# Layer 1's side work cut into steps of one or two f32 matmuls, beside a fixed 22-step unit of attention

## The chip, the cores and the metric

The kernel runs on one core of one Trainium2 chip. The metric is the device time of one execution in microseconds (us), as a median over runs.

## The reference, cut to what matters

Two layers work on x, 8 batches of 512 rows of 256 numbers. Layer 0 is softmax attention beside a mixture of experts. Layer 1 is two causal attentions with a convolution between them, beside a low-rank feed-forward part. The change is in layer 1's attention:

```python
qkv = x @ Wqkv_w.T + Wqkv_b
q, k, v = (qkv[:, :, 0], qkv[:, :, 1], qkv[:, :, 2])
ctx = _causal_attn(q, k, v)
conv_out = jax.lax.conv_general_dilated(ctx_c, conv_w, window_strides=(1,), padding=[(1, 1)], ...) + conv_b[None, :, None]
q2 = conv_out.transpose(0, 2, 1).reshape(b, s, NUM_HEADS, HEAD_DIM)
ctx2 = _causal_attn(q2, k, v)
out = ctx2.reshape(b, s, d) @ out_w.T + out_b
```

## The kernel before, in words

**Units.** Layer 1 is cut into 32 units, numbered 16 to 47. A unit is one batch, eight of the 16 heads (c = 0 or 1) and one of the two attentions: kind 1 is the first attention, kind 2 the second. The order is two units of kind 1, then two of kind 2, and so on. A unit has two halves (g = 0, 1) of four heads.

**What a unit needs.** Its queries and keys are computed as f32 matmuls (`query_key`, L765; for kind 2 the convolution, L1019, six matmuls of 512 columns) and its values (L773). ScalarE takes the bf16 head of each (`high`, L1607), VectorE the rest (`residue`, L1153), GpSimd splits that once more (L1844, L1846), and SyncE copies the parts by six DMAs into the tall tiles QA and KA (`fan`, L1986). For kind 1 the keys are also stored to DRAM (`ks`), from where kind 2 fans them again.

**The maxima.** The softmax subtracts each row's maximum before its exponentials. So a unit's scores are computed twice: first as packs into the three banks S1 (L804), where VectorE takes the maxima (L1195). The maxima of a half are transposed by TensorE (L811), split into three bf16 rows by VectorE (L1211 to L1219), and SyncE writes the rows into QA by three small DMAs from t_msp. Then the scores are computed again with these rows (L826, and L830 adds the causal mask) into the two banks S2, ScalarE takes the exponentials (L1629), and TensorE multiplies them by the values (`product`, L843) into the bank PV. A half is closed by a copy of PV (L1640), four transposes (L858) and a division (L1245, L1253).

**Stages.** One turn of `pipeline`'s loop, here called a stage, interleaves four lanes on every engine: `expp` of unit i (scores, exponentials, products, closings), `maxp` of unit i + 1 (maxima), `pre1` of unit i + 2 (queries, keys, values, fans), and `fin1` of unit i - 1 (for c = 1 of kind 2: transposes of the context, L724, the output projection, L1045, its addition, L1535, and the store). Every engine walks through the same lanes and emits only its own instructions, in this order; it waits at semaphores. `pre1` comes in every second step, `fin1` in every third. One step of `pre1` holds a whole `query_key`, a whole value projection or a whole convolution. A whole period is four stages, and this text names them by what `pre1` prepares: P and P (units of kind 1), Q (kind 2, c = 0, which has `fin1` beside it) and R (kind 2, c = 1).

**Waits that tie the stages.** TensorE's first pack of a unit waits in `maxp` for both fans of this unit (`d_f`); `pre1` issued them one stage earlier. The first scores of a half wait for the three rows of maxima (`d_mq`). SyncE issues all these DMAs in one order.

## Time and profile before

| | |
|---|---|
| median of 3 runs | 2157.86 us (2154.74 to 2158.21) |
| profiled execution, its own time | 2160.07 us |
| its span | 2158.2 us |
| mean granted TensorE clock | 0.935 |
| TensorE busy, VectorE busy, ScalarE busy | 85%, 58%, 47% of the span |
| layer 1's stages, from the first pack of the first to the end | 1223.5 to 2158.2 us |

The span is the time from the first to the last instruction of one profiled execution. Busy times of TensorE count each matmul to the end of its passage through the array, so that a busy TensorE is not one at its peak.

### The profile page before, as it was taken

What the parts mean: (1) busy time and instruction counts of PE and PEld (TensorE: products, weight loads), DVE (VectorE), ACT (ScalarE), POOL (GpSimd) and SP (SyncE); (2) the same over time, 40 slices, a digit from 0 to 9 for tenths busy, and PEclk for the clock granted to TensorE, in tenths of its full rate; (3) what the DMA queues carried; (4) which work ended last, traced back from release to release, by engine and by line L of the source; (5) the groups of instructions that cost most, each with busy time, mean ns of one, the idle gap of its engine ahead of it and who ended that gap; (6) DMA issues with size and microseconds to landing.
All of it is one profiled execution on the core that took longest, in us unless ns stands there. A gap on an engine that the chain in (4) does not pass through costs nothing.

```text
span 2158.2 us, 31797 instructions
## 1 busy us (share of the span) xinstructions
PE 1836.4 (85%) x10767; PEld 901.2 (42%) x10777; DVE 1255.3 (58%) x3777; ACT 1020.4 (47%) x2048; POOL 363.6 (17%) x555
## 2 busy tenths in 40 slices
PE   3475799999989999995489797998998898889987
PEld 2341344554534454541234343444444444444433
DVE  4554455655555444552554676767676767776663
ACT  0242456555545555564244244544454445445444
POOL 2215221121101111112443101001010100000000
PEclk8557899999999999998599899999999999999999
DMA  7245343434364444423104235555453545554350
GB/s 144 70 141 143 67 80 72 84 72 79 67 171 94 69 62 69 62 33 85 38 22 65 31 53 60 75 70 75 63 74 54 73 67 68 77 68 59 50 60 21
DMA packets 145969, 155.87 MB, mean 72 GB/s; under 512 B 26009, under 2 KB 132785, under 8 KB 145809
## 3 DMA queue, kind: packets, MB, share of 16 engines
q1 hardware_dynamic: 123872, 114.75, 34.0%
q0 software_dynamic: 10048, 14.44, 3.7%
q10 hardware_dynamic: 11888, 24.64, 3.6%
q8 instruction: 88, 1.44, 0.3%
q14 instruction: 73, 0.59, 0.1%
HBM read 55.95 MB, written 33.72 MB: 42 GB/s over the span
## 4 chain that ended last, share of the span: by engine, by line
PE 65%; DVE 15%; ACT 6%; issue 5%; DMA 4%; POOL 4%; SPq 2%; DVEq 0%; ACTq 0%; POOLq 0%
PE p_PV L843 12%; PE p_S L826 9%; PE p_S L804 9%; DVE p_S L1195 6%; PE p_Ma L1019 4%; PE p_Mb L898 4%; PE p_S L921 4%; ACT t_R L1629 3%; PE p_Ma L765 3%; SPq L1986 2%; PE p_Ma L773 2%; PE p_Mb L765 2%; PE p_S L830 2%; POOL idd L1878 1%; PE p_Mb L921 1%
## 5 line engine op out<-in xcount | busy, mean ns | idle before, releaser
L1629 ACT ACTIVATE t_R<-p_S 128x512 f32<-128x512 f32 (+1 forms) x1216 | 670.8, 577 | 503.7 <-PE p_S L830 347.0
L1195 DVE CUSTOM_DVE_ANT_0 p_S<-p_S,t_NM 128x128 f32<-128x128 f32 (+3 forms) x1024 | 472.3, 522 | 90.2 <-PE p_S L804 86.7
L804 PE MATMUL p_S<-t_R 96*128 96x512 bf16 (+3 forms) x1536 | 456.0, 340 | 64.2 <-DVE t_mx L1195 32.2
L1201 DVE TENSOR_REDUCE t_mx<-p_S 128x1 f32<-128x512 f32 x512 | 346.6, 686 | 260.1 <-PE p_S L804 247.0
L826 PE MATMUL p_S<-t_R 99*128 99x512 bf16 (+3 forms) x1536 | 468.4, 332 | 21.9 <-ACT t_R L1629 8.7
L843 PE MATMUL p_PV<-t_R 128*17 128x512 f32 (+3 forms) x3072 | 325.2, 495 | 12.4 <-ACT t_R L1629 10.0
L804 PEld LDWEIGHTS p_S<-t_R 96*128 96x128 bf16 x1536 | 135.8, 99 | 395.2 <-issue 136.5
L826 PEld LDWEIGHTS p_S<-t_R 99*128 99x128 bf16 x1536 | 150.0, 98 | 175.5 <-issue 79.6
L1844 POOL CAST t_spl<-t_rr 128x512 bf16<-128x512 f32 x80 | 49.0, 612 | 969.9 <-DVE t_rr L1153 969.8
L830 PE MATMUL p_S<-t_NM 128*128 128x128 bf16 x1024 | 196.1, 220 | 0.0
L1195 DVE DVE_READ_ACCUMULATOR2_ANT t_mx<- 128x1 f32 x1024 | 145.0, 142 | 0.0
L830 PEld LDWEIGHTS p_S<-t_NM 128*128 128x128 bf16 x1024 | 101.3, 99 | 37.8 <-issue 10.6
L898 PE MATMUL p_Mb<-t_R,t_NM 128*128 x184 | 97.9, 613 | 7.3 <-DMA t_NM<-hTd 3.0
L843 PEld LDWEIGHTS p_PV<-t_R 128*17 128x17 f32 x3072 | 50.9, 95 | 120.7 <-issue 86.1
L921 PE MATMUL p_S<-t_R,t_NM 128*128 x392 | 101.2, 380 | 0.0
L1846 POOL TENSOR_TENSOR t_spl<-t_rr,t_spl 128x512 bf16<-128x512 f32 x80 | 92.5, 1156 | 6.4
L1019 PE MATMUL p_Ma<-t_NM,t_R 128*128 128x512 f32 x192 | 90.4, 622 | 0.0
L921 PEld LDWEIGHTS p_S<-t_R,t_NM 128*128 128x128 f32 x392 | 74.3, 191 | 18.4 <-issue 2.9
L1211 DVE TENSOR_SCALAR t_msp<-p_S 16x128 bf16<-16x128 f32 x96 | 26.7, 278 | 74.6 <-PE p_S L811 71.5
L1902 POOL DMA_DIRECT2D ysd<-t_NM x39 | 34.1, 875 | 210.4 <-ACT t_NM L1688 210.4
L1153 DVE SCALAR_TENSOR_TENSOR t_rr<-p_Ma,t_BQK,t_spl 128x512 f32<-128x512 f32 x32 | 24.0, 751 | 76.2 <-ACT t_spl L1607 76.2
L1716 ACT ACTIVATE t_R<-p_S,t_R 128x512 f32<-128x512 f32 x64 | 43.5, 687 | 50.7 <-PE p_S L967 42.5
(245 smaller groups left out, 2124.1 us busy)
## 6 DMA issues: line engine op xcount, KB each, us to landing
t_R<-t_spl SPq DMA_DIRECT2D x480, 128.0 KB
t_R<-in_w ACTq DMA_DIRECT2D x32, 512.0 KB, 7.6
t_R<-ks SPq DMA_DIRECT2D x96, 128.0 KB
ks<-t_spl SPq DMA_DIRECT2D x16, 384.0 KB, 7.3
hTd<-t_NM SPq DMA_DIRECT2D x39, 128.0 KB
ysd<-t_NM SPq DMA_DIRECT2D x39, 128.0 KB
t_NM<-hTd SPq DMA_DIRECT2D x39, 128.0 KB, 2.3
ysd<-t_NM POOLq DMA_DIRECT2D x39, 128.0 KB, 3.1
```

The source lines that it names most:

```text
L765: t = self.nc.tensor.matmul(M[:, :], m.WQ[:, cc, off:off + 128], xT[:, cc, :], start=(cc == 0), stop=(cc == 1))
L804: t = self.nc.tensor.matmul(bank[:, z, :], qa[0:96, h, qb * 128:(qb + 1) * 128], ka[0:96, h, 0:n], start=True, stop=True)
L826: t = self.nc.tensor.matmul(bank[:, z, :], ka[0:99, h, kb * 128:(kb + 1) * 128], qa[0:99, h, n0:512], start=True, stop=not u.causal)
L830: t = self.nc.tensor.matmul(bank[:, z, 0:128], m.identb, m.maskk, start=False, stop=True)
L843: t = self.nc.tensor.matmul(m.PV[32 * j:32 * j + 17, n0:512], vt[:, kb, 4 * g + j, :], m.P1[kb][j] if u.causal else m.P[p % 2][:, j, :], s ...
L898: z = self.nc.tensor.matmul(m.MB[i][:, :], m.hT[t % 2][:, c, :], m.W1[:, bass.ds(self.regs[t], 1), c, :], start=(c == 0), stop=(c == 1))
L921: x = self.nc.tensor.matmul(M[:, 0:256], m.AT[:, k, :], m.W2[:, bass.ds(self.regs[t], 1), k * 256:k * 256 + 256], start=(k == 0), stop=(p ...
L1019: t = self.nc.tensor.matmul(M[:, :], m.CW[:, i, c * 128:c * 128 + 128], m.cT[:, cc, k:k + 512], start=(i == 0), stop=(i == 5))
L1195: x = nc.vector.tensor_tensor_reduce(out=sc, in0=sc, in1=m.maskq[:, 512 - n:512], scale=1.0, scalar=NEG, op0=ALU.add, op1=ALU.max, accum_o ...
L1201: nc.vector.tensor_reduce(m.mx[:, g, i:i + 1], m.S1[s1_bank(k)][:, :], AX.X, ALU.max).then_inc(s.s1_read, 1)
L1629: nc.scalar.activation(m.P1X[kb][j0 // per] if u.causal else m.P[p % 2][:, j0:j0 + per, :], m.s2_bank(k)[:, 0:per * n].rearrange("p (j n) ...
L1846: g.tensor_tensor(m.spl[:, z, 2, :], m.rr[:, :], m.spl[:, z, 1, :], ALU.subtract).then_inc(s.lo_done, 1)
```

## The change

`pipeline` goes. Now all four lanes take one part in each step, and a stage has 22 steps, one for each exponential: a pack of maxima and a piece of scores in every step. `pre1` starts at its step 3 (first step: 0) for kind 1 and gives one f32 matmul of `query_key` to a step (3, 4 and 6, 7), the value projection's eight small ones two to a step (10 to 13), the convolution's six one to a step (5 to 10 with the transposes ahead of it for c = 0, 3 to 8 for c = 1). `high1`, `rest` and `fan1` follow in the steps behind. The transposition of a half's maxima, its split and its rows (`shift`) come in steps 2 and 3 of the next half, where they stood in step 12 of their own half. The product of a block comes two steps after its last scores (`due`), and a half's closing (`close1`) in steps 2, 4 and 5 of the next half. `fin1` uses one bank for both of its transposes (Mb) and one for both of its projections (Ma). For the first batch of kind 2 and the last, `pre1` starts at step 6 and puts two matmuls of the convolution in a step; the two units that the feed-forward part prepares use the bank S1[2]. No operation is added or taken out.

```diff
-LATE2 = (4, 0, 0, 0, 0, 0, 0, 4)
-LATE = 3
...
+TOPS = {}
+_n = 0
+for _u in UNITS0:
+    for _g in range(2):
+        TOPS[_u.n, _g] = _n + len(packs_of(_u))
+        _n += len(packs_of(_u)) + 1
+for _u in UNITS1:
+    for _g in range(2):
+        _n += len(packs_of(_u))
+        TOPS[_u.n, _g] = _n + 2 * (_u.n - 16) + _g
+
+
+
+def bank_of(u, z):
+
+    return 2 if u.n < 18 else (0, 1, 0)[z]
...
 def layer1(e):
-    pipeline(UNITS1, 0, e.expp, e.maxp, e.pre1, lambda i, lane: [(lane(e.fin1, i - 1), 3)])
+
+    def lane(f, i):
+        return f(UNITS1[i]) if 0 <= i < len(UNITS1) else none()
+    for i in range(len(UNITS1) + 1):
+        interleave([(lane(e.expp, i), 1), (lane(e.maxp, i + 1), 1), (lane(e.pre1, i + 2), 1), (lane(e.fin1, i - 1), 1)])
 
...
-        return steps(s1_uses(u) + 2 * u.causal)
+        return self.maxima(u) if u.causal else self.maxp0(u)
+
+    def maxp0(self, u):
+        return steps(s1_uses(u))
+
+    def maxima(self, u):
+
+        for g in range(2):
+            for qb, js in packs_of(u):
+                self.top(u, g, qb, js)
+                next(self.chain, None)
+                yield
+            self.chain = self.shift(u, g)
+        if u.n == 47:
+            yield from self.chain
+
+    def shift(self, u, g):
+
+        yield
+        yield
+        self.turn_m(u, g)
+        self.split_m(u, g)
+        yield
+        self.rows(u, g)
+        yield
...
-        return steps(3 if u.kind == 1 else 2 if u.c else LATE2[u.b] + 4)
+
+        if u.kind == 1:
+            yield from steps(3)
+            self.part(u, 0, 0)
+            yield
+            self.part(u, 0, 1)
+            yield
+            self.high1(u, 0)
+            yield
+            self.rest(u, 0)
+            self.part(u, 1, 0)
+            yield
+            self.part(u, 1, 1)
+            yield
+            self.fan1(u, 0)
+            self.high1(u, 1)
+            yield
+            self.rest(u, 1)
+            yield
+            for k in range(4):
+                self.part(u, 2, k)
+                if k == 1:
+                    self.fan1(u, 1)
+                yield
+            self.values(u)
+            return
+        soon = u.c or u.b not in (0, NB - 1)
+        yield from steps(3 if u.c else 1 if soon else 6)
+        if u.c == 0:
+            for c in range(2):
+                self.turn_c(u, c)
+                yield
+                self.keep_c(u, c)
+                yield
+        for i in range(6):
+            self.convolve(u, i)
+            if i == 3:
+                self.fan1(u, 1)
+            if soon or i % 2:
+                yield
+        self.high1(u, 0)
+        yield
+        self.rest(u, 0)
+        yield
+        self.fan1(u, 0)
+        yield
...
-        return steps(LATE + 4) if u.kind == 2 and u.c else none()
+
+        if u.kind != 2 or u.c != 1:
+            return
+        yield from steps(6)
+        for c in range(2):
+            self.turn_f(u, c)
+            yield
+            self.keep_f(u, c)
+            yield
+        yield from steps(4)
+        for h in range(2):
+            self.out(u, h)
+            yield
+            self.add_out(u, h)
+            yield
+        self.store(u)
...
+    def exponentials(self, u):
+
+        for g in range(2):
+            for kb in range(4):
+                n0 = 128 * kb
+                per = (1, 1, 2, 4)[kb]
+                for j0 in range(0, 4, per):
+                    self.scores(u, g, kb, j0, per, n0)
+                    self.products()
+                    yield
+                self.due.append([2, u, g, kb])
+        if u.n == 47:
+            for _ in range(8):
+                self.products()
+                yield
+
+    def products(self):
+
+        for d in self.due:
+            d[0] -= 1
+        while self.due and self.due[0][0] == 0:
+            _, u, g, kb = self.due.pop(0)
+            self.product(u, g, kb)
+            if kb == 3:
+                self.closing = self.close1(u, g)
+        next(self.closing, None)
+
+    def close1(self, u, g):
+
+        yield
+        self.copy_o(u, g)
+        yield
+        yield
+        self.turn_o(u, g)
+        yield
+        self.divide(u, g)
+        yield
...
+    def top(self, u, g, qb, js):
+        e, m, s = self.e, self.m, self.s
+        qa, ka = m.QA[u.buf], m.KA[u.buf]
+        e.wait_ge(s.d_f[0][u.buf], 96 * u.fill)
+        e.wait_ge(s.d_f[1][u.buf], 96 * u.fill)
+        n = 128 * (qb + 1)
+        k, self.s1 = self.s1, self.s1 + 1
+        self.s1_free(k)
+        bank = m.S1[s1_bank(k)][:, 0:len(js) * n].rearrange("p (j n) -> p j n", j=len(js))
+        for z, j in enumerate(js):
+            h = 4 * g + j
+            t = self.nc.tensor.matmul(bank[:, z, :], qa[0:96, h, qb * 128:(qb + 1) * 128], ka[0:96, h, 0:n],
+                                      start=True, stop=True)
+        t.then_inc(s.s1_mm, 1)
+
+    def s1_free(self, k):
+
+        e, s = self.e, self.s
+        e.wait_ge(s.s1_read, k - 2 if k >= LAYER1 + 3 else LAYER1)
+        if k == LAYER1 + 1:
+            e.wait_ge(*self.mfree[2])
+        if k == LAYER1 + 2:
+            e.wait_ge(s.qs_done, NB)
+
+    def turn_m(self, u, g):
+        e, m, s = self.e, self.m, self.s
+        k, self.s1 = self.s1, self.s1 + 1
+        if u.causal:
+            self.s1_free(k)
+        e.wait_ge(s.s1_read, TOPS[u.n, g])
+        self.nc.tensor.transpose(m.S1[s1_bank(k)][0:16, 0:128], m.mx[:, g, :], m.ident[:, :]).then_inc(s.s1_mm, 1)
...
+    def part(self, u, z, k):
+        e, m, s, b = self.e, self.m, self.s, u.b
+        xT = m.XT[:, :, 512 * b:512 * b + 512]
+        i = bank_of(u, z)
+        if k == 0:
+            e.wait_ge(s.d_l2, 96)
+            e.wait_ge(s.nT_done, 2 * b + 2)
+            self.mbank(i, *((s.rr_done, QK[u.n, z]) if z < 2 else (s.v_done, VN[1, b, u.c])))
+        M = m.MB[i]
+        if z < 2:
+            off = 256 * z + 128 * u.c
+            t = self.nc.tensor.matmul(M[:, :], m.WQ[:, k, off:off + 128], xT[:, k, :], start=(k == 0), stop=(k == 1))
+            if k == 1:
+                t.then_inc(s.qk_mm, 1)
+        else:
+            off = 512 + 128 * u.c
+            for cc in range(2):
+                t = self.nc.tensor.matmul(
+                    M[:, k * 128:(k + 1) * 128], xT[:, cc, k * 128:(k + 1) * 128], m.WQ[:, cc, off:off + 128],
+                    start=(cc == 0), stop=(cc == 1))
+            if k == 3:
+                t.then_inc(s.v_mm, 1)
...
```

`convolve`, `turn_c`, `keep_c`, `turn_f`, `keep_f`, `out`, `add_out`, `store`, `split_m`, `rows`, `copy_o`, `turn_o`, `divide` hold the instructions of the old `pre1`, `fin1`, `maxp` and `close`.

**TensorE at the start of a stage P.** Before, with the wait for the rows of maxima in the first row (L826 scores, L830 mask, L804 maxima, L765 queries and keys, L843 products):

```order
L826 MATMUL p_S20<-t_R2 128x512 [waits d_mq20]
L830 MATMUL p_S20<-t_NM 128x128
L804 MATMUL p_S11<-t_R2 128x128 [waits d_f10,d_f00]
L804 MATMUL p_S11<-t_R2 128x128 x3
L765 MATMUL p_Ma<-t_R1,t_WQ 128x512 [waits rr_done]
L765 MATMUL p_Ma<-t_R1,t_WQ 128x512
L826 MATMUL p_S21<-t_R2 128x512 [waits s2_exp]
L830 MATMUL p_S21<-t_NM 128x128
L843 MATMUL p_PV<-t_R3,t_R1 17x128 x4
L804 MATMUL p_S12<-t_R2 128x256 x2
L804 MATMUL p_S10<-t_R2 128x256 [waits s1_read]
L804 MATMUL p_S10<-t_R2 128x256
```

In the changed kernel, from the third step's packs on (L999 scores, L1003 mask, L966 maxima, L985 transposition of maxima, L1179 queries and keys, L1026 closing):

```order
L966 MATMUL p_S12<-t_R2 128x256
L985 MATMUL p_S10<-t_ident,t_mx 16x128 [waits s1_read]
L999 MATMUL p_S21<-t_R2 128x512 [waits s2_exp]
L1003 MATMUL p_S21<-t_NM 128x128
L966 MATMUL p_S11<-t_R2 128x384 [waits s1_read]
L1179 MATMUL p_Ma<-t_R1,t_WQ 128x512 [waits rr_done]
L999 MATMUL p_S20<-t_R2 128x384 [waits s2_exp]
L1003 MATMUL p_S20<-t_NM 128x128
L1026 MATMUL p_Mb<-t_ident,t_O 128x128 [waits pv_read,ctx_done]
L1026 MATMUL p_Mb<-t_ident,t_O 128x128 x3
L966 MATMUL p_S12<-t_R2 128x512 [waits s1_read]
L1179 MATMUL p_Ma<-t_R1,t_WQ 128x512
```

The query's two matmuls moved from the first step to the fourth and fifth, with scores, a closing and a pack between them.

**TensorE at the end of a half and in the next one.** Before, the transposition of the maxima (L811) stands ahead of the last scores of its own half:

```order
L843 MATMUL p_PV<-t_R2,t_R1 17x384 [waits s2_exp]
L843 MATMUL p_PV<-t_R2,t_R1 17x384 x3
L811 MATMUL p_S10<-t_ident,t_mx 16x128 [waits s1_read]
L826 MATMUL p_S20<-t_R2 128x256
L830 MATMUL p_S20<-t_NM 128x128
L826 MATMUL p_S20<-t_R2 128x256
L830 MATMUL p_S20<-t_NM 128x128
L826 MATMUL p_S21<-t_R2 128x128 [waits s2_exp]
```

Now it stands behind the third pack of the next half (L1016 products):

```order
L1016 MATMUL p_PV<-t_R3,t_R1 17x128 x4
L966 MATMUL p_S11<-t_R2 128x256 [waits s1_read]
L966 MATMUL p_S11<-t_R2 128x256
L999 MATMUL p_S20<-t_R2 128x512 [waits s2_exp]
L1003 MATMUL p_S20<-t_NM 128x128
L966 MATMUL p_S12<-t_R2 128x256 [waits s1_read]
L966 MATMUL p_S12<-t_R2 128x256
L985 MATMUL p_S10<-t_ident,t_mx 16x128 [waits s1_read]
L999 MATMUL p_S21<-t_R2 128x512 [waits s2_exp]
```

The transposition waits for packs that were read three packs before it, and packs follow each other with no break.

**SyncE, the DMAs of a stage that prepares kind 2.** Before, the fan of the queries, then that of the keys from `ks`, then the rows of maxima:

```order
L1986 DMA t_R2<-t_spl 16x8x512 [waits pv_mm,lo_done]
L1986 DMA t_R2<-t_spl 16x8x512 x5
L1986 DMA t_R2<-ks 16x8x512 [waits d_ks]
L1986 DMA t_R2<-ks 16x8x512 x5
L1986 DMA t_R2<-t_msp 1x16x128 [waits msp_done]
L1986 DMA t_R2<-t_msp 1x16x128 x2
```

Now the keys' fan stands first:

```order
L2123 DMA t_R2<-ks 16x8x512 [waits pv_mm,d_ks]
L2123 DMA t_R2<-ks 16x8x512 x5
L2123 DMA t_R2<-t_spl 16x8x512 [waits lo_done]
L2123 DMA t_R2<-t_spl 16x8x512 x5
L2123 DMA t_R2<-t_msp 1x16x128 [waits msp_done]
L2123 DMA t_R2<-t_msp 1x16x128 x2
```

The fan of the queries stands directly ahead of the rows of maxima now. In a stage P the order of SyncE is as before.

## Rows read from the trace of the kernel before

**Rows 1.** Busy time (us, instructions), clock, DMA share and GB/s in one period: PE PEld DVE ACT POOL.

```profile
1803.90:1919.40 115.50, 104.08 (x786) 51.78 (x785) 79.95 (x314) 56.35 (x106) 10.60 (x12) 1.00 0.49 68
```

**Rows 2.** Timeline of TensorE: first packs of halves (start, length, instructions).

```profile
1803.93 0.39 PE L804 MATMUL p_S<-t_R 96*128 96x128 bf16 x4
...
1831.62 0.39 PE L804 MATMUL p_S<-t_R 96*128 96x128 bf16 x4
...
1859.23 0.39 PE L804 MATMUL p_S<-t_R 96*128 96x128 bf16 x4
...
1891.93 0.39 PE L804 MATMUL p_S<-t_R 96*128 96x128 bf16 x4
...
1919.44 0.39 PE L804 MATMUL p_S<-t_R 96*128 96x128 bf16 x4
```

**Rows 3.** Timeline of TensorE: what each kind of work takes.

```profile
1870.44 1.05 PE L843 MATMUL p_PV<-t_R 128*17 128x512 f32 x8
...
1872.04 0.60 PE L724 MATMUL p_Ma<-t_ident,t_NM 128*128 128x128 f32 x4
...
1891.64 0.39 PE L826 MATMUL p_S<-t_R 99*128 99x512 bf16 x1
1891.87 0.22 PE L830 MATMUL p_S<-t_NM 128*128 128x128 bf16 x1
...
1892.15 5.37 PE L1019 MATMUL p_Ma<-t_NM,t_R 128*128 128x512 f32 x12
```

**Rows 4.** Timeline of all engines: a query's way to its fan, stage P.

```profile
1803.65 0.39 PE L826 MATMUL p_S<-t_R 99*128 99x512 bf16 x1
...
1806.13 0.69 ACT L1607 ACTIVATE t_spl<-p_Ma,t_BQK 128x512 bf16<-128x512 f32 x1 [1.40 <-PE p_Ma L765]
...
1806.72 0.59 ACT L1629 ACTIVATE t_R<-p_S 128x512 f32<-128x512 f32 x1
1806.85 0.75 DVE L1153 SCALAR_TENSOR_TENSOR t_rr<-p_Ma,t_BQK,t_spl 128x512 f32<-128x512 f32 x1 [1.39 <-ACT t_spl L1607]
...
1808.36 1.16 POOL L1846 TENSOR_TENSOR t_spl<-t_rr,t_spl 128x512 bf16<-128x512 f32 x1
...
1809.54 2.53 SPq L1986 DMA_DIRECT2D t_R<-t_spl  x4
```

**Rows 5.** Timeline of SyncE's DMA issues in the second stage P.

```profile
1837.22 9.21 SPq L1986 DMA_DIRECT2D t_R<-t_spl  x12
...
1847.89 12.46 SPq L1986 DMA_DIRECT2D t_R<-t_msp  x6
```

**Rows 6.** The tile t_msp, 1847 to 1851 us: its three DMAs.

```profile
DMA to landing us min/median/max: 3.9/4.1/4.3
```

**Rows 7.** The tile t_msp, 1855 to 1862 us, with no fan in the queue.

```profile
DMA to landing us min/median/max: 1.6/1.7/1.7
```

**Rows 8.** TensorE's waits, 1342 to 2035 us (six periods): total, times, longest.

```profile
PE p_S L804 <- DVE t_mx L1195: 20.3, 42, 0.6
PE p_Mb L858 <- DVE t_rr L1153: 16.8, 12, 1.4
PE p_Mb L1045 <- DVE t_R L1253: 9.7, 6, 1.6
```

**Rows 9.** Timeline of TensorE: a late fan, and the first packs around it.

```profile
2034.95 0.39 PE L804 MATMUL p_S<-t_R 96*128 96x128 bf16 x4
...
2068.68 0.59 PE L804 MATMUL p_S<-t_R 96*128 96x128 bf16 x4 [5.85 <-DMA t_R<-ks]
2069.06 8.12 PE L1019 MATMUL p_Ma<-t_NM,t_R 128*128 128x512 f32 x12
...
2099.09 0.39 PE L804 MATMUL p_S<-t_R 96*128 96x128 bf16 x4
```

**Rows 10.** Busy time and granted clock around that wait.

```profile
2064.00:2066.00 2.00, 0.00 (x0) 0.00 (x0) 0.00 (x0) 0.00 (x0) 0.00 (x0) 0.59 1.15 123
```

424 lines of the change are left out of this document (172 added, 252 removed).

## The prediction

> **What bounds the kernel now.** I read busy times by stretch first, then the timeline of TensorE for the stages' lengths, then its waits, and last SyncE's queue. A period of four stages takes 115.5 us, with TensorE busy for 104.1, VectorE for 80.0, ScalarE for 56.4, the clock at its full 2.4 GHz [rows 1]. The first packs of the stages stand at 1803.93, 1831.62, 1859.23, 1891.93 and 1919.44 [rows 2]: P 27.7, P 27.6, Q 32.7, R 27.5 us. Layer 1 has six such periods (1342 to 2035) and eight stages around them.
>
> How much of that does TensorE need? Scores of 512 columns start 0.23 us ahead of the mask, the mask 0.06 ahead of the next row, four maxima of 128 columns take 0.22, six f32 matmuls of 512 columns 5.37, so 0.87 each with the tail off, the products of a block of 512 columns 1.05 (0.98 without the tail), four transposes 0.60 (0.44 without) [rows 2, 3]. A half has 5120 columns of maxima (2.2 us), as many of scores with 16 masks (3.1), products of 1280 columns by four at a time (2.6), a closing (0.44) and a transposition (0.1): 8.45, a unit 16.9. A stage P adds a query, a key (1.74 each) and values (1.8, by column count): 22.2. Q adds the convolution (5.2), 16 transposes (1.8) and the output's f32 matmuls (3.5, by column count): 27.4. R adds the convolution: 22.1. Together 93.9 of 115.5 us: TensorE is the bound, and 21.6 us a period are waits and gaps. VectorE's 80.0 fit under 93.9, so it binds only locally: a half without side work needs 8.45 of TensorE and about 80.0/8 = 10 of VectorE. The named waits that I can sum over six periods are TensorE on the maxima 20.3, on the residue ahead of a closing 16.8, on the division ahead of the projection 9.7 us [rows 8]; the rest are small gaps, and those in which VectorE starves while five us of f32 matmuls run.
>
> **What the change gives.** With a pack in every step and at most two f32 matmuls between packs, VectorE is fed evenly. The wait for the residue goes, since the closing no longer stands right behind the key's residue on bank Mb. The transposition of maxima waits for packs three steps old. From these alone I would take the stages at 5% over TensorE's work, P 23.6 (a little more, as its first half has VectorE's split on its heels), Q 28.9, R 23.6. What holds them longer is SyncE's queue.
>
> **What it costs: the fans come later.** TensorE's first pack of the next stage waits for both fans that this stage issued, and the first scores for the rows of maxima behind them. Before, the query's matmuls come in step 0: scores at 1803.65, ScalarE's head 1806.13, residue 1806.85 to 1807.60, GpSimd's two operations to 1809.52, SyncE at 1809.54 [rows 4]. So the fan starts 5.9 us into the stage. From the first of twelve fan DMAs (1837.22) to the last row of maxima landed it is 15.8 us: the three rows are issued from 1847.89, 0.59 apart, and land 3.9 us or more after issue, the last at about 1853.0 [rows 5, 6]. 5.9 + 15.8 = 21.7, of 27.6: hidden, with 6 us to spare.
>
> Now the query's second matmul stands in step 4. TensorE, step by step from the rows above: step 0 scores 0.28, products of 256 columns 0.56, packs 0.22; step 1 0.84; step 2 0.60 with the transposition; step 3 0.28 + 0.17 + 0.87; step 4 0.22 + 0.44 + 0.22 + 0.87. That ends at 5.6. ScalarE first takes the exponential of step 5 (0.59), then the head (0.69): 7.2. VectorE takes the residue behind the pack of step 6, whose matmul stands behind a product of 0.98: it starts at 8.2 and ends at 9.0. GpSimd's two operations end at 11.0 (1.92 with the handover), SyncE starts at 11.2 [rows 3, 4]. The key's fan is ready at 14.3, before the query's six issues are done, so the twelve and the store to `ks` follow each other with no gap longer than that in [rows 5]: 11.2 + 15.8 = 27.0. **P: 27.1**, against 27.65. The stage gives up 5.3 us of side work's lead and gets back almost nothing.
>
> R: the convolution's last matmul is in step 8, at 11.8 us by the same count; head to 13.5, residue behind the pack of step 10 to 15.4, GpSimd to 17.3, SyncE at 17.4. Only six DMAs now lie ahead of the rows; the keys' fan went out early. The six issues take 3.6 us, three rows 1.8; below, the rows land 1.7 us after that, as from an empty queue [rows 7], so at 7.1; above, they wait for the six transfers: 8.7 (half of 15.8, and 0.8). I take 8.0, since fans keep the queue longer than their issues: **R: 25.4** against 27.5. Q: the last matmul is in step 10 behind the transposes, SyncE at 21.6, rows at 29.6. TensorE needs 28.9: **Q: 29.6** against 32.7.
>
> A period is then 2 x 27.1 + 29.6 + 25.4 = 109.2, 6.3 less; six of them: -38.
>
> **The other stages.** The stage R at 2068.68 loses 5.85 us to a late fan, and then runs with a fallen clock: the convolution takes 8.12 instead of 5.37 us [rows 3, 9]. It lasts 30.4 and the Q before it 33.7; the first Q and R of layer 1 are of the same build, and I price them alike. With the fans as above, R should be near 25.4: twice 5, so -10, and +1 for caution with the first. The two stages Q have the convolution in steps 10 to 12 and the fan at 22 to 24: 31 to 32.5, -3.5. The last stage but one has no fans and goes by VectorE: -4. The first two stages P -1. The start: VectorE's clearing of PV no longer stands behind the split of the maxima: -1.8. The end: out of one bank, the second transposes and the second projection wait for the copy and the addition before them, +1.8. The two units prepared in the feed-forward part share one bank for three projections: +1. Sum -16.5.
>
> **The clock.** Where TensorE waited 5.85 us, its clock went to 1.2 GHz about 1.4 us into the wait (mean 0.59 over 2064 to 2066, the wait from 2062.83) and cost 2.75 us of the convolution behind it [rows 3, 9, 10]. The new stages P end in a wait of 27.1 - 23.6 = 3.5 us. Waits up to 1.6 us left the clock up [rows 1, 8]; between 1.6 and 5.8 nothing is shown. The bounds: it never falls in 14 stages P (0), or always (14 x 2.7 = 38). I take one in three: +13. The Trainium skill ("TensorE: Matmul & The Clock Gate", Why this matters for your kernels) warns of idle gaps between bursts of matmuls, after which the engine is back at half rate; the fall in the trace agrees with it. By that rule alone, with the clock fallen at every boundary, this would be no gain at all; see the third rival.
>
> One more rule is weighed. The rows of maxima are 12 KB behind megabytes, and in this trace they land long after issue, 4.1 against 1.7 us [rows 6, 7]. The Trainium skill ("DMA: Bandwidth & Descriptors", Queues, rings and completion order) says that descriptors of one ring start in order but completion is not first in, first out. If the rows passed the store to `ks`, P would end 1.2 us sooner, 17 us over 14 stages; the 4.1 us of the trace speak against it, and the sum goes by the trace.
>
> **Sum.** The profiled execution took 2160.07 us, 2.2 over the median of 2157.86; against the median: -38 - 16.5 + 13 = -41.5, so **2116 us**.
>
> **Rivals.** (1) The fans don't bind, because the queue drains sooner than reckoned (the twelve DMAs are then spread, and the first six ran alone in [rows 5]). P 23.6, Q 28.9, R 23.6 give 99.7, -15.8 a period, -95 and some -27 around: about 2036 us. For it speaks that TensorE's work is only 93.9; against it the 15.8 us of [rows 5, 6], measured from issue to landing. (2) The change doesn't do what it says: fans and clock eat it whole, P and R at their old 27.6, Q gained back at the end: within 0.2% of 2158. For it speaks that P is but 0.5 us below its old length. (3) Slower: the clock falls at nearly every boundary. The slow first matmuls then push the query's end from 5.6 to about 8.5 us, the fan by 3 us, the wait stays long and the clock falls again. P 30.1, Q 32.6, R 28.4: 121.2, +5.7 a period, 2190 us. One such fall costs 3 us of a stage; the 54.5 us that the rest saves are gone at 18 falls in 30 stages. For it speaks the fall after 1.4 us [rows 10]; against it that a wait of 3.5 us is not one of 5.9.
>
> **Chances.** The forecast (2090 to 2150, with some falls of the clock) 0.60, rival (1) 0.17, (2) 0.08, (3) 0.15. A measurement of this kernel can tell 0.2% (4.3 us) from no change. Faster 0.77, same 0.08, slower 0.15. Range: 2060 to 2165, into the upper part of (1), with fans binding half of the time, and the lower of (3).
>
> **What would show it.** In the changed trace: the first fan of a stage P issued 11 us after the stage's first scores; TensorE's first scores or packs of a stage waiting on a DMA, 3 us in P and 1 to 2 in R; stages of 27, 27, 29.6, 25.4; the waits on the residue and for the transposed maxima gone; the clock line with slices under 9 if it falls. It would be wrong if no DMA wait stands at the boundaries (then 2036), or if the clock's mean in layer 1 goes below 0.9 (then 2160 or more).

## The result, and the profile after

The changed kernel takes 2187.43 us (median of 4 runs, 2184.19 to 2191.29), the kernel before beside it 2158.03: a ratio of 1.0133, 95% interval 1.0102 to 1.0163. It is 1.3% slower; I had forecast 2116. The profiled execution took 2186.33 us, with a span of 2184.5.

The page of the kernel after, three of its lines: busy times, the granted clock in 40 slices (tenths), and the shares of the chain that ended last.

```profile
PE 1857.6 (85%) x10767; PEld 920.8 (42%) x10777; DVE 1256.4 (58%) x3777; ACT 1023.8 (47%) x2048; POOL 363.3 (17%) x555
...
PEclk8557899999989999997799899998999999999999
...
PE 56%; SPq 11%; DVE 10%; DMA 10%; issue 4%; POOL 4%; ACT 2%; another core or an unknown queue 1%; DVEq 0%; POOLq 0%; ACTq 0%
```

The busy shares are those of before, so they don't show where the time went. What changed is who is waited for. TensorE's waits over 1342 to 2035 us of the kernel after, the same stretch as [rows 8] (total us, times, longest):

```profile
PE p_S L999 <- DMA t_R<-t_msp: 65.4, 23, 4.4
PE p_Ma L885 <- ACT t_NM L1902: 4.5, 6, 0.9
PE p_S L966 <- DVE t_mx L1375: 2.1, 10, 0.2
PE p_Ma L1226 <- DVE t_rr L1333: 1.6, 6, 0.3
```

The 20.3 us on the maxima are 2.1, the 16.8 on the residue ahead of a closing and the 9.7 on the division are gone: 45 us of waits removed, as the change should. In their place stand 65.4 us of a wait that the kernel before did not have in this stretch: the first scores of a stage on the rows of maxima. The busy times and the clock (the column ahead of the last two) over the six periods say the rest:

```profile
1338.20:2063.80 725.60, 646.43 (x4708) 327.96 (x4706) 484.81 (x1884) 341.08 (x636) 63.57 (x72) 0.93 0.44 65
```

A period is 120.9 us where it was 115.5 [rows 1], and the mean clock is 0.93 where it was full. The stages by their first packs are P 29.9 on average, Q 33.4, R 27.8 (before 27.7, 32.7, 27.5). The six periods are 32.6 us longer; everything else together is 6.3 us shorter, 5.5 of which lie ahead of layer 1, whose start moves by as much from run to run (1215.9 to 1224.2 in the runs below).

TensorE's timeline in the kernel after, the first scores (L999) and first packs (L966) of five stages P, P, Q, R, P:

```profile
1576.86 0.61 PE L999 MATMUL p_S<-t_R 99*128 99x512 bf16 x1 [2.56 <-DMA t_R<-t_msp]
...
1578.49 0.61 PE L966 MATMUL p_S<-t_R 96*128 96x128 bf16 x4
...
1607.39 0.61 PE L999 MATMUL p_S<-t_R 99*128 99x512 bf16 x1 [3.66 <-DMA t_R<-t_msp]
...
1637.99 0.61 PE L999 MATMUL p_S<-t_R 99*128 99x512 bf16 x1 [3.71 <-DMA t_R<-t_msp]
...
1671.20 0.39 PE L999 MATMUL p_S<-t_R 99*128 99x512 bf16 x1 [1.02 <-DMA t_R<-t_msp]
...
1698.82 0.39 PE L999 MATMUL p_S<-t_R 99*128 99x512 bf16 x1 [3.27 <-DMA t_R<-t_msp]
...
1700.00 0.61 PE L966 MATMUL p_S<-t_R 96*128 96x128 bf16 x4
```

Read the second column: 512 columns of scores take 0.39 us at the full clock and 0.61 at half. Behind the waits of 2.56, 3.66 and 3.71 us they take 0.61; behind the wait of 1.02 they take 0.39; and behind that of 3.27 the first matmul is still fast and the packs 1.2 us later (0.40 at the full clock) are not. The same in windows (length, busy times, clock, DMA share, GB/s) around the first and the fourth of these boundaries:

```profile
1576.00:1577.00 1.00, 0.14 (x1) 0.13 (x2) 0.00 (x0) 0.00 (x0) 0.00 (x0) 0.79 0.00 0
1577.00:1578.00 1.00, 1.00 (x10) 0.15 (x8) 0.00 (x0) 0.39 (x1) 0.00 (x0) 0.50 0.00 0
...
1582.00:1584.00 2.00, 2.00 (x6) 0.97 (x5) 1.90 (x9) 0.97 (x2) 0.00 (x0) 0.65 0.00 0
1584.00:1586.00 2.00, 2.00 (x16) 1.17 (x17) 1.19 (x6) 0.49 (x1) 0.00 (x0) 1.00 0.02 4
...
1671.00:1672.00 1.00, 0.80 (x10) 0.25 (x10) 0.00 (x0) 0.32 (x1) 0.00 (x0) 1.00 0.09 30
1672.00:1674.00 2.00, 2.00 (x26) 1.20 (x23) 1.43 (x11) 1.09 (x3) 0.00 (x0) 1.00 0.00 0
```

I went through all 30 boundaries of layer 1 at which TensorE waits for a DMA in this way. At 25 of them the clock is at 1.2 GHz in the wait or behind it; it stays up behind the four waits of up to 1.12 us and one of 2.72. It falls at no fixed time: from 1.8 to 4.6 us behind the start of the wait, and so in part only after the wait has ended.

Then SyncE's queue in the kernel after (start, issue time of the group, count): a stage P, a stage Q, a stage R.

```profile
1591.08 7.72 SPq L2123 DMA_DIRECT2D t_R<-t_spl  x12
1598.84 0.60 SPq L2123 DMA_DIRECT2D ks<-t_spl  x1
1599.49 1.81 SPq L2123 DMA_DIRECT2D t_R<-t_msp  x3
...
1662.19 3.81 SPq L2123 DMA_DIRECT2D t_R<-t_spl  x6
1666.05 2.30 SPq L2123 DMA_DIRECT2D t_R<-t_msp  x3
...
1689.14 3.82 SPq L2123 DMA_DIRECT2D t_R<-t_spl  x6
1693.01 1.86 SPq L2123 DMA_DIRECT2D t_R<-t_msp  x3
```

P: the first fan (1591.08) comes 14.2 us after the stage's first scores at 1576.86, and the rows have landed 16.3 us after it, at 1607.39 (over the twelve stages P of the six periods 11.6 to 14.3, and 15.6 to 17.0). Q: the fan 24.2 after 1637.99, the rows landed 9.0 later. R: 17.9 after 1671.20, and 9.7 (9.0 to 9.7 over the six stages R). From these I set up the experiments: the fans are late, and the clock makes them later.

### The profile page after: what moved, and what is told of

Read it like the earlier page. It is cut to its first block, busy times and chain, and to the rows that moved or that the text cites. A ratio compares the mean times of both kernels' runs of the same rounds, so it can differ in the third digit from the quotient of the medians.

```text
span 2184.5 us, 31852 instructions
## 1 busy us (share of the span) xinstructions
PE 1857.6 (85%) x10767; PEld 920.8 (42%) x10777; DVE 1256.4 (58%) x3777; ACT 1023.8 (47%) x2048; POOL 363.3 (17%) x555
## 4 chain that ended last, share of the span: by engine, by line
PE 56%; SPq 11%; DVE 10%; DMA 10%; issue 4%; POOL 4%; ACT 2%; another core or an unknown queue 1%; DVEq 0%; POOLq 0%; ACTq 0%
SPq L2123 11%; PE p_PV L1016 9%; PE p_S L999 8%; DMA t_R<-t_msp 6%; PE p_S L949 5%; PE p_Ma L1204 4%; PE p_S L966 4%; PE p_Mb L1066 4%; PE p_S L1089 4%; DVE p_S L1375 2%; POOL t_spl L1996 2%; DVE t_mx L1361 2%; PE p_Mb L1089 1%; DMA t_xTb<-xTd 1%
## 5 line engine op out<-in xcount | busy, mean ns | idle before, releaser
L1792 ACT ACTIVATE t_R<-p_S 128x512 f32<-128x512 f32 (+1 forms) x1216 | 683.6, 577 | 666.0 <-PE p_S L1003 512.2
L1375 DVE CUSTOM_DVE_ANT_0 p_S<-p_S,t_NM 128x128 f32<-128x128 f32 (+3 forms) x1024 | 483.6, 511 | 308.4 <-PE p_S L966 300.4
L999 PE MATMUL p_S<-t_R 99*128 99x512 bf16 (+3 forms) x1536 | 488.1, 342 | 94.7 <-DMA t_R<-t_msp 80.4
L1016 PE MATMUL p_PV<-t_R 128*17 128x512 f32 (+3 forms) x3072 | 337.6, 514 | 1.1 <-ACT t_R L1792 1.0
L966 PE MATMUL p_S<-t_R 96*128 96x128 bf16 (+3 forms) x1024 | 275.5, 325 | 20.3 <-DMA t_R<-t_spl 10.7
L999 PEld LDWEIGHTS p_S<-t_R 99*128 99x128 bf16 x1536 | 153.4, 100 | 233.4 <-DMA t_R<-t_msp 89.8
L949 PE MATMUL p_S<-t_R 96*128 96x512 bf16 x512 | 205.8, 405 | 19.7 <-DVE t_mx L1361 17.9
L1003 PE MATMUL p_S<-t_NM 128*128 128x128 bf16 x1024 | 205.7, 226 | 0.0
L966 PEld LDWEIGHTS p_S<-t_R 96*128 96x128 bf16 x1024 | 87.6, 104 | 211.0 <-DVE t_mx L1375 91.0
L1003 PEld LDWEIGHTS p_S<-t_NM 128*128 128x128 bf16 x1024 | 104.7, 102 | 72.9 <-issue 44.9
L1016 PEld LDWEIGHTS p_PV<-t_R 128*17 128x17 f32 x3072 | 51.8, 97 | 125.3 <-issue 123.1
L1204 PE MATMUL p_Ma<-t_NM,t_R 128*128 128x512 f32 x192 | 98.4, 598 | 0.0
L1089 PEld LDWEIGHTS p_S<-t_R,t_NM 128*128 128x128 f32 x392 | 73.7, 190 | 17.9 <-issue 2.3
```

Source lines behind the costliest of these rows:

```text
L949: self.nc.tensor.matmul(m.S1[s1_bank(k)][:, :], qa[0:96, 4 * g + j, qb * 128:(qb + 1) * 128], ka[0:96, 4 * g + j, 0:512], start=True, stop ...
L966: t = self.nc.tensor.matmul(bank[:, z, :], qa[0:96, h, qb * 128:(qb + 1) * 128], ka[0:96, h, 0:n], start=True, stop=True)
L999: t = self.nc.tensor.matmul(bank[:, z, :], ka[0:99, h, kb * 128:(kb + 1) * 128], qa[0:99, h, n0:512], start=True, stop=not u.causal)
L1003: t = self.nc.tensor.matmul(bank[:, z, 0:128], m.identb, m.maskk, start=False, stop=True)
L1016: t = self.nc.tensor.matmul(m.PV[32 * j:32 * j + 17, n0:512], vt[:, kb, 4 * g + j, :], m.P1[kb][j] if u.causal else m.P[p % 2][:, j, :], s ...
L1089: x = self.nc.tensor.matmul(M[:, 0:256], m.AT[:, k, :], m.W2[:, bass.ds(self.regs[t], 1), k * 256:k * 256 + 256], start=(k == 0), stop=(p ...
```

## The experiments

All times are medians; the ratio is to the kernel before, with its 95% interval.

| run | what | us | ratio |
|---|---|---|---|
| after | the change | 2187.4 | 1.0133 (1.0102 to 1.0163) |
| early_p | kind 1's pre1 at step 0 | 2147.4 | 0.9944 (0.9927 to 0.9962) |
| early_pr | c = 1 of kind 2 too | 2119.5 | 0.9808 (0.9785 to 0.9832) |
| warm | after, 12 matmuls in each long wait | 2153.0 | 0.9973 (0.9962 to 0.9985) |
| warm4 | after, 4 of them | 2174.7 | 1.0076 (1.0063 to 1.0090) |
| before_late | before, kind 1's pre1 later | 2139.4 | 0.9915 (0.9897 to 0.9932) |
| rows_act | after, rows on ScalarE's queue | 2155.0 | 0.9989 (0.9977 to 1.0000) |
| half_bytes | after, half the bytes in Q and R | 2169.1 | 1.0054 (1.0038 to 1.0070) |
| half_bytes_p | after, half the bytes in P | 2149.1 | 0.9962 (0.9947 to 0.9977) |
| one_bank | early_pr, kind 1 on Ma alone | 2102.3 | 0.9748 (0.9734 to 0.9761) |
| ks_last | one_bank, the store behind the rows | 2092.1 | 0.9701 (0.9686 to 0.9715) |
| q_pairs | one_bank, Q's convolution in pairs | 2090.5 | 0.9679 (0.9663 to 0.9696) |
| both | ks_last and q_pairs | 2076.4 | 0.9618 (0.9605 to 0.9631) |
| warm_ends | both, matmuls in two waits | 2072.6 | 0.9603 (0.9589 to 0.9616) |

**Earlier fans, in P.** Against the changed kernel:

```diff
         if u.kind == 1:
-            yield from steps(3)
             self.part(u, 0, 0)
...
             self.rest(u, 0)
+            yield
+            yield
+            self.fan1(u, 0)
             self.part(u, 1, 0)
...
-            self.fan1(u, 0)
             self.high1(u, 1)
...
-    return 2 if u.n < 18 else (0, 1, 0)[z]
+    return 2 if u.n < 18 else (0, 0, 1)[z]
```

> The changed kernel with one edit: for kind 1, pre1 starts at step 0 instead of 3 (query's matmuls in steps 0 and 1, its fan from step 5 instead of 8; the key's matmuls in steps 5 and 6 instead of 6 and 7, now on bank Ma; values on Mb one step earlier). Theory 1, late fans plus the clock's falls: in the changed kernel a stage P has its first fan 12.8 us after its first scores and the last row of maxima landed 15.8 us after that. Here the first fan should come at about 8.5 us and the rows be landed at 24.5, near TensorE's own 23.6; the wait at the end of P shrinks from 3.3 to 1 us or less and the clock stays up at most of these boundaries: P 25 instead of 29.9, 14 stages, about 2115 to 2130. Theory 2, the cutting of the side work into single steps is what costs (f32 matmuls between packs, bank switches), fans do not matter: within 0.5% of 2187. Theory 3, fans earlier than this only move the wait (the twelve DMAs land when they did): same stages as in the changed kernel, 2187.

2147.4: 40 us less than the changed kernel, so theories 2 and 3 are out; but it is 17 us above my range. TensorE's waits of this run over 1342 to 2035 us, the two largest:

```profile
PE p_S L1000 <- DMA t_R<-t_msp: 24.9, 14, 3.1
PE p_Mb L1027 <- DVE t_R L1351: 20.5, 12, 1.7
```

The wait for the rows went from 65.4 to 24.9. The second line is mine: the closing's transposes now wait 1.7 us in each stage P for the values' addition on bank Mb, where I had put the values.

**Earlier fans, in R too.**

```diff
-        yield from steps(3 if u.c else 1 if soon else 6)
+        yield from steps(0 if u.c else 1 if soon else 6)
```

> As the run before, and pre1 of kind 2, c = 1, starts at step 0 instead of 3 as well (convolution in steps 0 to 5, fan from step 8). Theory 1: the fan of a stage R comes 3 steps, some 3.2 us, sooner, so the 3 us wait at its end goes and so does the fall of the clock behind it: R 24 to 24.5 instead of 27.9, eight stages, 20 to 25 us less than the run before, about 2095 (2080 to 2110), below both kernels. Theory 2: as the run before, 2187.

2119.5, 28 us less than the run before it, though 9.5 above my range. It is below both kernels, with all of the change's interleaving in it. Its wait for the rows is 10.2 us in the same stretch, that on Mb 20.6.

**The clock by itself.** The next run leaves every fan where the change put it, and gives TensorE something to do in the wait:

```diff
+        if g == kb == j0 == 0 and 17 <= u.n < 46 and (v.kind == 1 or v.c):
+            e.wait_ge(s.masks, 6)
+            for _ in range(12):
+                self.nc.tensor.matmul(m.s2_bank(k)[:, 0:512], m.identb, m.maskq, start=True, stop=True)
         e.wait_ge(s.d_mq[u.buf][g], 48 * u.fill)
```

> The changed kernel, and TensorE runs 12 extra bf16 matmuls of 512 columns (identity times the mask) into the bank of scores just ahead of its wait for the rows of maxima, at every stage boundary behind a stage P or R; their result is overwritten by the scores. At the full clock they take 2.6 us, inside a wait of 3 to 4 us. Theory 1 says that the wait alone costs what I forecast (P 27.1) and the rest is the clock: with the clock kept up at 22 boundaries, the query's matmuls end 1.5 us sooner after the first scores, the fan comes at 11.2 instead of 12.8, P 27.1 to 27.5 instead of 29.9, R 26 instead of 27.9: about 2125 to 2140, though the matmuls take nothing away from the DMAs. If the clock is not the cause (the waits would be the same with the clock up) the time stays at 2187 or rises by up to 2.6 us a boundary where the wait is shorter.

The edit reaches 21 boundaries, not the 22 of the expectation. 2153.0: 34 us less by adding 55 us of matmuls. TensorE's timeline of this run at a boundary, its busy times and clock over six periods, and its wait for the rows over 1342 to 2035 us:

```profile
1594.65 2.32 PE L1000 MATMUL p_S<-t_NM 128*128 128x512 bf16 x10
1598.19 0.39 PE L1004 MATMUL p_S<-t_R 99*128 99x512 bf16 x1 [1.22 <-DMA t_R<-t_msp]
...
1341.10:2032.20 691.10, 652.56 (x4907) 334.06 (x4922) 481.02 (x1884) 340.55 (x637) 63.66 (x72) 1.00 0.47 68
...
PE p_S L1004 <- DMA t_R<-t_msp: 23.9, 21, 2.3
```

The clock is full in all six periods, and these take 691.1 us instead of 725.6: the whole difference of the two kernels. So the fallen clock is worth 34.5 us here, 1.8 for each of the 19 falls in these periods of the changed kernel. But the time is 13 to 28 us above what I expected: with the clock up, P is 27.9 (forecast 27.1), R still 27.4 (25.4) and Q 31.9 (29.6), each a mean over the six periods. Something besides the clock holds the stages, Q and R above all.

With four matmuls in place of twelve:

> As warm, with 4 extra matmuls instead of 12 ahead of the wait at the same 22 boundaries of the changed kernel: 0.9 us of work, so that of waits of 2.6 to 4.2 us 1.8 to 3.4 stay idle. In the changed kernel waits of 1.8 us and more had a fallen clock behind them at 25 of 26 boundaries and those under 1.2 us at none. If the idle time is what counts, most falls stay and the time is near the changed kernel's, 2170 to 2187; if any work in the wait is enough to keep the clock, it is warm's 2153.

2174.7, in the range and nearer to the changed kernel than to warm: the clock fell behind 18 of its 30 waits. Waits over 1.7 us are on both sides there (2.65 without a fall, 1.73 with one); behind the six under 1.7 the clock never fell. Less idle time means fewer falls, and in between its length alone does not decide.

**The kernel before, with later fans.** To see whether the fans' place costs anything by itself:

```diff
+    def later(i):
+        if i < len(units) and units[i].kind == 1:
+            yield from steps(3)
+        yield from lane(pre, i)
...
-        interleave([(lane(expp, i), 1), (lane(maxp, i + 1), 1), (lane(pre, i + 2), every)] + extra(i, lane))
+        interleave([(lane(expp, i), 1), (lane(maxp, i + 1), 1), (later(i + 2), every)] + extra(i, lane))
```

> The kernel before, with one edit: in the loop of layer 1, pre1 of kind 1 starts three of its own steps (six steps of a unit) later; all else as before. Theory 1: the query's fan of a stage P starts about 13 us into the stage instead of 5.9, the last row of maxima lands at 29, past the 27.6 of the stage: a wait of 1.5 us or more on the rows of maxima at 14 boundaries, and where it is long enough the clock falls, 3 us each: 2190 to 2230 (wait alone 2180). Theory 2, fans are irrelevant and the cutting costs: 2158.

2139.4: faster, and both theories were wrong. The first scores of a stage P of this run, its fan, the next stage's first scores, and TensorE's wait for the rows over 1342 to 2035 us:

```profile
1447.16 0.39 PE L832 MATMUL p_S<-t_R 99*128 99x512 bf16 x1
...
1456.62 7.74 SPq L1992 DMA_DIRECT2D t_R<-t_spl  x12
...
1473.43 0.39 PE L832 MATMUL p_S<-t_R 99*128 99x512 bf16 x1
...
PE p_S L832 <- DMA t_R<-t_msp: 0.8, 2, 0.4
```

Six steps at a stage's start are short; the fan moved from 5.9 to 9.5 us behind the first scores, not to 13. That uses up 3.6 of the 6 us that [rows 4 to 6] left to spare, and the rows are still in time (0.8 us of waits in all). And the wait on the residue [rows 8] is gone, since the key's matmuls no longer stand ahead of a closing: P takes 26.4 on average instead of 27.6. A fan up to the edge costs nothing. Beyond it, it costs the wait, and where the wait is long enough the clock on top.

**What the rows of maxima wait for.** In the changed kernel they stand behind 12 (P) or 6 (Q, R) fans in SyncE's queue. Here ScalarE issues them:

```diff
+    def rows_act(self, u, g):
...
+        for x in range(3):
+            self.raw.dma_start(m.QA[u.buf][96 + x:97 + x, 4 * g:4 * g + 4, :], m.msp[:, x, :]).then_inc(s.d_mq[u.buf][g], 16)
```

> The changed kernel, with the three rows of maxima issued by ScalarE, on its own queue and one step later, instead of by SyncE behind the fans. Theory 1, the queue is what makes the end of a stage: in the changed kernel's stage P the first fan is issued at 12.8 us, the last fan at some 21, the rows land at 28.6; without the rows behind them the last fan should be landed 4.5 us after its issue, 3 us sooner than the rows did, and in R and Q about 1.9 us sooner. The waits fall under 2 us, most falls of the clock go: 2125 (2105 to 2150). Theory 2, the transfers and not the places in the queue take the time (fans land when the rows landed): 2175 to 2190. ScalarE pays six issues a stage; if these delay its exponentials, up to 1 us a stage of it comes back.

2155.0: above my range, between the theories. In a stage P of this run, SyncE's and ScalarE's issues, how long the rows of maxima took from issue to landing, and the first scores behind them:

```profile
1576.31 7.70 SPq L2133 DMA_DIRECT2D t_R<-t_spl  x12
1583.57 2.06 ACTq L1896 DMA_DIRECT2D t_R<-t_msp  x3
...
DMA to landing us min/median/max: 7.7/7.7/8.0
...
1592.72 0.39 PE L1001 MATMUL p_S<-t_R 99*128 99x512 bf16 x1 [3.29 <-DMA t_R<-t_msp]
```

With the 1.6 to 1.7 us of an idle queue [rows 7] they would have landed at 1587; they land at 1592.7, 16.4 us after the first fan, as in the changed kernel (16.3). This trace also has the landings of the fans (the tile t_R, 1576.30 to 1583.45 us: the twelve fans of this stage):

```profile
DMA to landing us min/median/max: 3.3/5.8/8.2
```

The first fan lands 3.3 us after its issue, the last 15.1 us after that same moment: one fan is issued every 0.64 us, but one lands only every 1.07. Over the groups of this run that had no other fan in transfer ahead of them, six fans take 8.4 to 8.8 us from the first issue to the last landing, and twelve 14.0 to 15.3. The rows land right behind the last fan. So in this stage it is not the place in the queue that holds them, it is the DMA engines. Over the twelve stages P the rows take 14.2 to 16.7 us, 15.7 on average against 16.2 in the changed kernel: ScalarE's queue gives 0.5 us. The Trainium skill ("DMA: Bandwidth & Descriptors", Issuing engines are not separate DMA queues) says that DMAs of any issuing engine run on the same 16 engines and interleave there, so that a second issuer saves only its sequencer's time; here the trace agrees. In R the rows do land sooner, 8.1 us after the first fan in place of 9.7 in the stages shown, and the stages R and Q are 1.4 and 1.1 us shorter on average. With shorter waits there the clock falls behind fewer of them (its mean over the six periods is 0.96 in place of 0.93), and the stages P behind them have their fans earlier: 27.9 us in place of 29.7 from first scores to first scores, which is 21 of the 36 us that this run gains in the six periods.

So bytes were the next thing to halve, first in Q and R, then in P:

```diff
+            if u.kind == 2 and z == 0:
+                self.start(to[16 * j:16 * j + 8, :, :], part[0:64], s.d_f[z][u.buf])
```

> The changed kernel, and the query's six fan DMAs of kind 2 (stages Q and R) copy 8 of their 16 rows each: as many DMAs, half the bytes. It leaves out half of the copying of the second attention's queries, so their scores are of stale rows. In the changed kernel the rows of maxima land 9.0 to 9.7 us after this fan's first issue, where I forecast 8.0 from six issues at 0.6, three at 0.6 and a landing. If the bytes make it (768 KB at the 120 to 180 GB/s of these stretches are 4 to 6 us behind the issues), the rows land about 2 us sooner, the waits at the ends of Q and R shrink by as much, Q and R are 1 to 2 us shorter: 2160 to 2175. If the issues and the landing's own time make it, nothing moves: 2187.

> The changed kernel, and the twelve fan DMAs of kind 1 (12 of the 14 stages P) copy 8 of their 16 rows each: as many DMAs, half the bytes of the fans. It leaves out half of the copying of the first attention's queries and keys, so their scores are of stale rows. Rows of maxima on ScalarE's own queue landed no sooner in P (16.4 us behind the first fan against 16.3), at 7.1 us and more after their issue. If the bytes set that time (2.0 MB at about 120 GB/s), then with 1.2 MB the rows should land some 12.6 us behind the first fan (twelve issues 7.7, the store 0.6, three rows 1.8, a landing of 2.5), the waits of 3 us at the ends of P all but go, the clock stays up there, P lasts 24 to 25 instead of 29.9: 2187 - 12 x 5.4 = about 2122 (2110 to 2135). If the number of DMAs in the queue sets it: 2180 to 2187.

2169.1 and 2149.1: the first in its range, the second 14 us above it. The fan and the first scores that its rows release, R of the first run and P of the second:

```profile
1683.28 3.99 SPq L2123 DMA_DIRECT2D t_R<-t_spl  x6
...
1691.81 0.39 PE L999 MATMUL p_S<-t_R 99*128 99x512 bf16 x1 [2.13 <-DMA t_R<-t_msp]
```
```profile
1576.53 8.21 SPq L2123 DMA_DIRECT2D t_R<-t_spl  x12
...
1590.47 0.39 PE L999 MATMUL p_S<-t_R 99*128 99x512 bf16 x1 [1.29 <-DMA t_R<-t_msp]
```

The six stages R take 8.1 to 8.5 us from fan to rows instead of 9.0 to 9.7, about 1 us less where I expected 2; the twelve stages P 13.5 to 15.0, on average 14.4, instead of 15.6 to 17.0, on average 16.2, where I expected 12.6. Halving the bytes takes off 1 us in R and some 2 in P, and not more, because something else sets the pace then. The busy share of the DMA engines shows it (tenths in 40 slices of 17 us from a stage P's first fan; first the changed kernel, then with half the bytes):

```profile
DMA  0007699999999999999999999999999989410000
...
DMA  0004243454555565575557996654420000000000
```

With all the bytes the engines are busy throughout, and the transfers set the pace. With half of them the engines are about half idle until the store comes. The issues, one each 0.65 to 0.7 us, are then the likely pace; the profile has no landing of a single fan there that would show it. P took 26.8 us and not 24 to 25, and the clock still fell at 18 of 30 waits, and that leaves the run above its range.

**Towards a better version.** The run one_bank takes my new wait away:

```diff
-    return 2 if u.n < 18 else (0, 0, 1)[z]
+    return 2 if u.n < 18 else 0
```

> The early version (pre1 at step 0 for kind 1 and for c = 1 of kind 2), with query, key and values of kind 1 all on bank Ma and the values in steps 10 to 13, so that the closings have Mb alone. In the run before it the closing's transposes waited 1.7 us for the values' addition on Mb in every stage P. Expected: that wait gone, stages P at 25 to 25.6 instead of 26.2, now set by the fans (first fan 9.8 us after the first scores, 15.8 to the last row landed): 2119.5 - 14 x 0.8 = about 2108 (2100 to 2116). If the fans bind at 26.2 already: 2119.

2102.3, in its range; the wait on Mb for the values is gone from the list. P takes 25.9 us, and the wait for the rows is back in its place: 24.5 us over 1342 to 2035, after 10.2 in early_pr. Then the store of the keys behind the rows:

```diff
-        if u.kind == 1 and z == 1:
+        if u.kind == 1 and z == 1 and u.n < 18:
             self.start(m.ks[2 * u.b + u.c], m.spl[:, 1, :, :], s.d_ks)
...
             self.start(m.QA[u.buf][96 + x:97 + x, 4 * g:4 * g + 4, :], m.msp[:, x, :], s.d_mq[u.buf][g])
+        v = UNITS1[u.n - 15] if 17 <= u.n < 47 else u
+        if g == 0 and v.n >= 18 and v.kind == 1:
+            self.start(m.ks[2 * v.b + v.c], m.spl[:, 1, :, :], s.d_ks)
```

> As one_bank, and the store of the key's parts to ks stands behind the rows of maxima in SyncE's queue instead of ahead of them. In the rows of the kernel before, this store's issue takes 0.6 us and its 384 KB some 2 us of transfer. If descriptors go in the order of the queue, the rows land 0.6 to 2 us sooner and P, if the fans bind there, is as much shorter: 2090 to 2100. If rows pass the store anyway, or TensorE binds in P: no difference to one_bank.

2092.1, 10 us less. The queue of a stage P in this run, and the first scores behind it:

```profile
1468.44 10.24 SPq L2125 DMA_DIRECT2D t_R<-t_spl  x12
1478.72 1.88 SPq L2125 DMA_DIRECT2D t_R<-t_msp  x3
1480.64 0.58 SPq L2125 DMA_DIRECT2D ks<-t_spl  x1
...
1483.79 0.39 PE L1001 MATMUL p_S<-t_R 99*128 99x512 bf16 x1 [0.20 <-DMA t_R<-t_msp]
```

The wait at this end of P is 0.2 us; over 1342 to 2035 the waits for the rows went from 24.5 to 15.1 us, and a stage P ends 15.5 us after its first fan instead of 16.4. The prediction had weighed whether rows pass a store that stands ahead of them. In the changed kernel's stage P above the first of the rows did: the store, issued at 1598.84, took 8.0 us to land, the rows, issued from 1599.49 on, 6.5 to 6.8. But to have the store ahead was not free.

Then Q's convolution, two matmuls to a step:

```diff
-            if soon or i % 2:
+            if u.c or i % 2:
                 yield
```

> As one_bank, and in stages Q the convolution's matmuls go two to a step (steps 5 to 7 instead of 5 to 10), so that the fan comes three steps, some 3.3 us, sooner. In the early version Q still lasts 31.9 us, where TensorE's own work is 27.4, and its rows land at the end. If the late fan holds Q: 29.5 instead of 31.9 in six stages, 12 to 15 us less than one_bank, about 2094. If VectorE, starved by pairs of f32 matmuls or loaded by the split, holds Q: no difference.

2090.5: the late fan held Q, not VectorE. It now comes 19.9 us into the stage instead of 22.8, and Q takes 30.2 instead of 32.0. Both edits together:

> ks_last and q_pairs together on top of one_bank. Alone they took 10 and 12 us off 2102; they act in different stages (the store in P, the pairs in Q), so together 2080 (2076 to 2086). If they act through the same waits: 2088 to 2090.

2076.4, in its range and 3.8% below the kernel before. The gains of 10 and 12 us alone became 26 together, so the two edits at least add up. The six periods of this run:

```profile
1331.50:1962.20 630.70, 609.42 (x4708) 310.58 (x4704) 482.77 (x1884) 334.98 (x637) 63.58 (x72) 1.00 0.51 75
```

A period is 105.1 us at the full clock, TensorE busy for 101.6 of it. Last, the two waits of 5.3 us at the boundaries behind the late stages Q:

```diff
+        if u.kind == 2 and u.c == 0 and u.b in (0, NB - 1) and g == 0 and (qb, js) == packs_of(u)[0]:
+            for _ in range(20):
+                self.nc.tensor.matmul(m.S1[s1_bank(k)][:, 0:512], m.identb, m.maskq, start=True, stop=True)
         e.wait_ge(s.d_f[0][u.buf], 96 * u.fill)
```

> As both, and 20 extra bf16 matmuls of 512 columns (4.3 us at the full clock) ahead of TensorE's wait for the fans at the two boundaries behind the late stages Q, where it waits 5.3 us and the clock falls. There nothing but the clock can change: with 1.7 to 2.8 us of full clock lost behind each of the two waits, 3 to 5.5 us less than both (2075 to 2077 against 2080); if the price of a fall is hidden by VectorE, no difference.

2072.6. It is 3.8 us less, as expected, but the two intervals overlap; the size is not settled. The profile shows that the wait shrank and that the packs behind it run at the full clock (four in 0.40 us); the first row is the end of the 20:

```profile
1984.79 1.03 PE L965 MATMUL p_S<-t_NM 128*128 128x512 bf16 x4
1986.71 0.40 PE L971 MATMUL p_S<-t_R 96*128 96x128 bf16 x4 [0.89 <-DMA t_R<-t_spl]
```

## Why the prediction was wrong

**What held.** TensorE bounds the kernel, and with its 93.9 us of work a period there was room: the run called both reached 105.1. The waits on maxima and residue went as foretold, that on the division with them. The mechanism against the change was the named one: late fans, rows of maxima landing behind them, 15.8 us in P (15.6 to 17.0 measured), and a wait at the stage's end. The query's fan of P at the full clock starts at 11.6 in warm, 11.2 forecast.

**The steps that failed.** The forecast for the six periods was 109.2 each, 655 us, without the clock; they took 725.6. The run warm, with the clock up, took 691.1, and so splits these 70 us in two: 34.5 for the clock and 36 for the rest.

First, "The clock: ... I take one in three: +13". It fell at 25 of 30 boundaries, also at the ends of R and Q, where I had counted no fall. That is 34.5 us in these periods (2153 against 2187 in the medians), where 13 were forecast for all of layer 1. Rival (3) named this, with stages of 30.1, 32.6 and 28.4; measured are 29.9, 33.4 and 27.8, and its time of 2190 is 3 us off. That closeness is luck in part: it charged 3 us for each fall, 12 a period where 5.8 were measured, and had the period without the falls 6 us too short (109.2 against 115.2), so that two errors cancel. I gave it 0.15 because waits of 3.5 us had no row: shown were 1.6, without a fall, and 5.9, with one. I put my value near the lower end although the fall itself, in [rows 10], came 1.5 us into the wait (the prediction says 1.4; the mean of 0.59 over 2064 to 2066 puts it at 2064.36, the wait began at 2062.83). Nor was this row a rule. The kernel before has a second such wait, from 1306.28 to 1312.19, which the prediction prices but does not read:

```profile
1306.00:1310.00 4.00, 0.28 (x2) 0.00 (x0) 0.00 (x0) 0.60 (x1) 0.00 (x0) 1.00 1.15 124
1310.00:1312.00 2.00, 0.00 (x0) 0.00 (x0) 0.00 (x0) 0.00 (x0) 0.00 (x0) 0.50 0.30 27
```

There the clock fell 3.7 us into the wait. With both read, falls in waits of 3.5 us were open in either direction, and one in three had nothing behind it. The price of a fall was mis-sized the other way: 1.8 us a fall measured, 2.7 to 3 forecast. A mean clock of 0.93 over 725.6 us is some 50 us of full clock lost, and 34.5 of them cost time. Why the rest did not is not shown; part of it lies in the waits themselves, where TensorE has nothing to do.

Second, "I take 8.0" for six fans and the rows, between 7.1 and 8.7. Measured are 9.0 to 9.7, above my upper bound, which was half of P's 15.8. But P's 15.8 is no sum of twelve equal pieces: in rows_act the first fan lands 3.3 us after its issue and the others about 1.05 us apart, so that six alone take 8.4 to 8.8 us, more than I had for them and the rows. At the full clock (warm) R took 27.4 instead of 25.4, 0.5 of it because the fan itself came at 17.9 and not at 17.4. In Q the fan came at 22.8 instead of 21.6, and Q took 31.9 instead of 29.6. With 0.8 in each P (its fan 0.4 late, its rows 16.4 us behind it instead of 15.8) this makes the other 36 us.

Third, the other stages. I had priced the two boundaries behind the late Q at -5 each. The waits there are 5.34 and 5.40 us and were 5.91 and 5.85, so almost nothing was gained: the fan of the late Q comes 26.1 us into its stage, where I had 22 to 24. Of the -16.5, at most 6.3 came, and most of those lie ahead of layer 1.

**The cutting itself** is not at fault: the run called both has the same interleaving and is 3.8% faster than before. What cost in P and R was the late place of `pre1`: three steps of delay ahead of it, in a stage whose last transfer had 6 us to spare. Early_p and early_pr show it, together -68 us from the changed kernel's 2187 (early_p also moves the key's matmuls and fan a step earlier, and the banks).

**What stays open.** Why the clock stays up behind some waits between 1.4 us (a fall in rows_act) and 2.7 us (none at one boundary of the changed kernel) and falls behind others isn't settled. Nor is what sets the first fan's 3.3 us from issue to landing, or why in some stages P of rows_act the rows land after 14.2 us and in others after 16.7.
